# Two-layer attention with experts and feed-forward: row maxima as pairs of half-height matmuls

## The reference, cut to what matters

```python
q = (hidden_states @ Wq.T + bq).reshape(B, N, H, D).transpose(0, 2, 1, 3)
k = (encoder_hidden_states @ Wk.T + bk).reshape(B, T, H, D).transpose(0, 2, 1, 3)
...
scores = jnp.einsum('bhnd,bhtd->bhnt', q, k) * scale + attention_mask[:, None, :, :]
attn = jax.nn.softmax(scores, axis=-1)
...
attn_score = jnp.einsum('bhid,bjd->bhij', qh, k) / np.sqrt(D_HEAD)
attn_prob = jax.nn.softmax(attn_score, axis=-1)
```

## Time and profile before

| | |
|---|---|
| median of 3 runs | 789.1 us (788.37 to 789.65) |
| the profiled execution | 788.65 us, of which the span is 786.4 us |
| PE busy | 730.7 us (93%) |
| DVE busy | 645.4 us (82%) |
| ACT busy | 513.6 us (65%) |
| POOL busy | 374.3 us (48%) |
| granted TensorE clock, mean | 0.99 |
| row maxima on DVE, L342 | 256 operations, 108.6 us busy |
| row maxima on PE, L388 and mask L391 | 81.2 us and 37.7 us busy |

### The profile page before, as it was taken

The page is one execution under the profiler, slowest core; times in us unless marked ns, Lnnn a source line. Parts: engine busy times, 40 slices in busy tenths (PEclk is TensorE's granted clock), DMA queues, the critical chain, the costliest instruction groups (busy, mean ns, idle before and its releaser), DMA issues.

```text
span 786.4 us, 13553 instructions
## 1 busy us (share of the span) xinstructions
PE 730.7 (93%) x4372; PEld 548.4 (70%) x4372; DVE 645.4 (82%) x1546; ACT 513.6 (65%) x943; POOL 374.3 (48%) x323
## 2 busy tenths in 40 slices
PE   4799999999999999999998999999989999999995
PEld 3456666766558888888875555555558888888985
DVE  7658778777878878888887888998788999999995
ACT  3546556565654456555436777677778989989885
POOL 6374444334222223232214232222259999999884
PEclk9999999999999999999999999999999999999999
DMA  7975635564210000001047755755200000000001
GB/s 231 135 208 121 143 71 96 119 120 87 69 36 1 1 1 7 1 1 55 1 60 121 92 78 77 131 76 78 32 1 1 2 28 28 28 28 2 28 28 54
DMA packets 25101, 48.64 MB, mean 62 GB/s; under 512 B 3686, under 2 KB 7016, under 8 KB 24520
## 3 DMA queue, kind: packets, MB, share of 16 engines
q1 hardware_dynamic: 23366, 46.54, 30.6%
q10 hardware_dynamic: 1666, 1.24, 0.5%
HBM read 12.12 MB, written 4.19 MB: 21 GB/s over the span
## 4 chain that ended last, share of the span: by engine, by line
PE 53%; DVE 20%; issue 9%; ACT 7%; DMA 6%; POOL 4%; DVEq 0%; ACTq 0%; POOLq 0%
PE bank L141 15%; PE bank L649 7%; PE bank L413 6%; PE bank L436 6%; DMA qst<-mt 5%; PE bank L424 5%; PE bank L388 4%; DVE mx L342 4%; PE bank L416 3%; PE bank L812 3%; DVE fpart L768 3%; DVE x L617 2%; PE bank L391 2%; DVE fyl L780 2%; POOL fy L728 2%
## 5 line engine op out<-in xcount | busy, mean ns | idle before, releaser
L316 ACT ACTIVATE pt<-bank 77x512 f32<-77x512 f32 x256 | 141.0, 589 | 79.1 <-PE bank L416 59.3
L342 DVE TENSOR_REDUCE mx<-bank 128x4 f32<-128x308 f32 x256 | 108.6, 470 | 22.9 <-PE bank L391 12.3
L413 PE MATMUL bank<-qst,l_kst 128*77 128x512 f32 (+1 forms) x256 | 102.6, 416 | 16.8 <-DMA qst<-mt 10.5
L721 POOL TENSOR_TENSOR frise<-fg,fg 128x512 f32<-128x512 f32 x64 | 101.8, 1591 | 6.0 <-DVE fpart L768 0.8
L388 PE MATMUL bank<-l_kblk,qh 128*128 128x308 f32 x256 | 81.2, 339 | 7.6 <-DVE mx L342 6.4
L284 POOL TENSOR_TENSOR ol<-ot,oh 128x512 fp32r<-128x512 f32 x32 | 41.4, 1293 | 94.5 <-ACT oh L321 50.4
L103 POOL TENSOR_TENSOR rstd<-var,minus_half 128x4 f32<-128x4 f32 x32 | 34.8, 1088 | 102.5 <-DVE var L98 54.4
L617 DVE SCALAR_TENSOR_TENSOR x<-bank,eweight,x 128x256 f32<-128x256 f32 x192 | 79.5, 475 | 4.5 <-PE bank L649 4.2
L413 PEld LDWEIGHTS bank<-qst,l_kst 128*77 128x77 f32 (+1 forms) x256 | 36.5, 146 | 66.0 <-ACT pt L316 24.1
L114 ACT ACTIVATE xn<-x,shift,rstd 128x256 f32<-128x256 f32 (+1 forms) x128 | 67.0, 592 | 17.9 <-POOL shift L105 17.9
L812 PE MATMUL bank<-fw2h,fyh 128*128 128x256 f32 x256 | 73.3, 286 | 5.0 <-DVE fyl L780 4.7
(11 more groups left out here) (176 smaller groups left out, 2115.6 us busy)
## 6 DMA issues: line engine op xcount, KB each, us to landing
qst<-qh SPq DMA_DIRECT2D x64, 256.0 KB, 6.5
qst<-ql SPq DMA_DIRECT2D x32, 256.0 KB, 8.7
out<-x SPq DMA_DIRECT2D x8, 512.0 KB, 2.6
qst<-ml SPq DMA_DIRECT2D x8, 480.0 KB
x<-in_x SPq DMA_DIRECT2D x3, 1024.0 KB, 12.7
weights<-in_mlp_w SPq DMA_DIRECT2D x2, 1024.0 KB, 5.2
mraw<-in_mask SPq DMA_DIRECT2D x8, 154.0 KB
x<-in_x SPq DMA_DIRECT2D x2, 512.0 KB, 5.4
```

Of the source, the lines that this page charges most:

```text
L316: self.nc.scalar.activation(self.pt[0:T, i // 4 % 2, i % 4, :], self.bank_of(G, i)[0:T, :], ACT.Exp).then_inc(self.probs, 1)
L342: self.nc.vector.reduce_max(out, banks[u % len(banks)][:, 0:4 * T].rearrange("q (p par t) -> q p par t", p=2, par=2), AX.X).then_inc(self. ...
L413: last = self.nc.tensor.matmul(out, layer.kst[rows, layer.stack(c * HC + 2 * k + par), b * T:(b + 1) * T], self.qst[rows, self.slot(G), c ...
L721: self.nc.gpsimd.tensor_tensor(self.rise[:, k % 2, :], self.g1[:, k % self.R, :], self.g0[:, k % self.R, :], ALU.subtract).then_inc(self.r ...
```

## The change

`max_pair` replaces `max_unit`. Pair v (8 in a block) is row tile t and slab c. It makes two matmuls of 64 rows each, one on the rows 0 to 63 and one on the rows 64 to 127, each of 308 columns and 128 columns of weights, into the two banks of a double tile of PSUM. In the built program the two carry the array tile (64, 128) at row 0 and row 64; the bias row and the anchors carry (32, 128). In layer 0 two mask matmuls on all rows follow. One `reduce_max` takes both banks, 616 columns a row. There is only one double tile in the steady blocks (`X`), so pair v waits until pair v - 1 is taken; two in blocks 0 and 8. The constant `headsel` changes with the order of the heads.

The orders are new on PE, DVE and ACT. On PE in layer 0: both queries at i = 1, the weigh of the block before at i = 3 (was 1), the outputs at 11 (was 10), the third weigh at 14 (was 15), `hidden` of the experts at 12 and 15 (was 10 and 14). In layer 1: the queries of slab 0 before score 0, the weigh of the block before at i = 1, the first weigh at 6, both turns at 12. On DVE in layer 1 `fold` of slab 0 comes behind the small parts of the norm.

```diff
-        for u in units:
-            t, c, half = u // 4, u % 4 // 2, u % 2
-            dve.wait_ge(self.max_scores, 16 * G + u + 1)
...
+        for v in units:
+            t, c = divmod(v, C)
+            dve.wait_ge(self.max_scores, 8 * G + v + 1)
...
+            out = self.mx[:, t, :].rearrange("q (par c p) -> q c par p", par=2, c=C)[:, c, :, :]
+            self.nc.vector.reduce_max(out, banks[v % len(banks)][:, :, 0:4 * T].rearrange("q par (p t) -> q par p t", t=T),
                                       AX.X).then_inc(self.max_taken, 1)
...
+        if v >= len(banks):
+            pe.wait_ge(self.max_taken, 8 * G + v - len(banks) + 1)
+        pair = banks[v % len(banks)]
+        tile = slice(t * P, (t + 1) * P)
+        for par in range(2):
+            half = slice(64 * par, 64 * par + 64)
+            last = self.nc.tensor.matmul(pair[:, par, 0:4 * T], self.qh[half, c, tile],
+                                         layer.kblk[half, c % layer.kc, self.batch(G), 4 * par:4 * par + 4, :],
+                                         start=True, stop=not layer.masked)
+        if layer.masked:
+            for par in range(2):
+                last = self.nc.tensor.matmul(pair[:, par, 0:4 * T], self.mh[:, tile], self.id5[:, 0:4 * T], start=False, stop=True)
         last.then_inc(self.max_scores, 1)
...
+        self.X = (pair,)
...
+        PAIRS0 = {2: 0, 3: 1, 6: 2, 8: 4, 11: 5}
+        PAIRS1 = {1: 0, 4: 2, 6: 3, 7: 4, 10: 5, 11: 7}
+        FIRST_MAX = (double[2], double[6])
+        FIRST_MAX1 = (double[6], double[2])
...
                     if n < 2 * BLOCKS:
-                        att.take_maxima(dve, n, range(6, 10), att.X)
+                        att.take_maxima(dve, n, range(3, 4), att.X)
+                        att.rest(dve, n, 1)
+                        att.take_maxima(dve, n, range(4, 5), att.X)
...
-                    att.fold(dve, G, 0)
                     if nm <= LN_FFN:
                         for c in range(C):
                             norm.rest(dve, nm, c, att.W[c], att.xh if nm < LN_FFN else ff.xh[0], att.xl if nm < LN_FFN else ff.xl[0])
+                    att.fold(dve, G, 0)
...
-                        if i == 15:
+                        if i == 14:
                             att.weigh(pe, l0, G, 2)
-                        if i in (10, 14) and n == BLOCKS:
-                            if i == 10:
+                        if i in (12, 15) and n == BLOCKS:
+                            if i == 12:
...
+                        if i == 0 and BLOCKS < G and n < 2 * BLOCKS:
+                            att.queries(pe, l1, n, 0)
                         att.score(pe, l1, G, i)
+                        if i == 0 and G == BLOCKS:
+                            att.queries(pe, l1, n, 0)
                         if i == 1 and n < 2 * BLOCKS:
-                            for c in range(C):
-                                att.queries(pe, l1, n, c)
-                        if i == 5:
+                            att.queries(pe, l1, n, 1)
+                        if i == 6:
                             att.weigh(pe, l1, G, 0)
```

More of the change, by code:

```diff
@@ L376, in queries, with max_pair @@
         self.norm.project(self.W[c][:, :], layer.wqh, layer.wql, slice(c * P, (c + 1) * P), self.xh, self.xl).then_inc(self.q_done, 1)
-    def max_unit(self, pe, layer, G, u, banks):
-        t, c, half = u // 4, u % 4 // 2, u % 2
+    def max_pair(self, pe, layer, G, v, banks):
+        t, c = divmod(v, C)
         pe.wait_ge(self.qh_ready, C * G + c + 1)
[L381 to L388, removed]
         if layer.masked:
             pe.wait_ge(self.mask_ready, 3 * G + 1)
-            last = self.nc.tensor.matmul(bank, self.mh[:, tile], self.id5[:, 0:4 * T], start=False, stop=True)
+        if v == 0:
+            need(pe, self.mt_ready, G)
+        if v >= len(banks):
[10 more added lines that the diff above has]
+                last = self.nc.tensor.matmul(pair[:, par, 0:4 * T], self.mh[:, tile], self.id5[:, 0:4 * T], start=False, stop=True)
         last.then_inc(self.max_scores, 1)
     def turn_maxima(self, pe, G, bank):
-        pe.wait_ge(self.max_taken, 16 * (G + 1))
+        pe.wait_ge(self.max_taken, 8 * (G + 1))
         for t in range(NT):
@@ L846, in sem @@
             return stack.enter_context(nc.semaphore(n))
-        ps = [stack.enter_context(nc.psum_tensor(f"bank{i}", [P, N], F32)) for i in range(8)]
+        single = {i: stack.enter_context(nc.psum_tensor(f"bank{i}", [P, N], F32)) for i in (0, 1, 4, 5)}
+        double = {i: stack.enter_context(nc.psum_tensor(f"bank{i}{i + 1}", [P, 2, N], F32)) for i in (2, 6)}
+        ps = [single[i][:, :] if i in single else double[i - i % 2][:, i % 2, :] for i in range(8)]
         x = place.at("x", m["x"], [P, BLOCKS * NT, D], F32)
@@ L1406, in _ @@
                         att.rest(dve, n, 0)
[L1407 to L1408 removed]
+                        att.take_maxima(dve, n, range(0, 1), att.X)
                     if p >= BLOCKS:
@@ L1673, in _ @@
                         if i == 12 and n < 2 * BLOCKS:
-                            att.turn_maxima(pe, n, att.X[0])
-                        if i in (12, 13) and nm <= LN_FFN:
-                            if p >= BLOCKS:
-                                pe.wait_ge(att.added, 2 * p + i - 11)
-                            else:
-                                pe.wait_ge(att.ql_ready, C * n + i - 11)
-                            norm.turn(pe, nm, i - 12, att.W[i - 12])
+                            att.turn_maxima(pe, n, ps[2])
+                        if i == 12 and nm <= LN_FFN:
+                            for c in range(C):
+                                if p >= BLOCKS:
+                                    pe.wait_ge(att.added, 2 * p + c + 1)
+                                else:
+                                    pe.wait_ge(att.ql_ready, C * n + c + 1)
+                                norm.turn(pe, nm, c, att.W[c])
                         if i == 14:
```

149 lines of the change are left out of this document (71 added, 78 removed).

## The result

The changed kernel takes **811.6 us** (median of 4 runs, 810.12 to 813.9) against 788.89 for the kernel before (788.37 to 789.65): a ratio of 1.029, interval 1.0263 to 1.0317. The forecast said 793 and 782 to 804, so the sign is right and the loss, 22.7 us, is more than five times the 4 us forecast. The profiled execution has a span of 807.9 us against 786.4. The mean granted clock is 0.969, where it was 0.99; the prediction has no word on the clock.

What follows compares the result with a forecast made beforehand. PE was taken to bound layer 0, and PE's work plus 2.6 us of waits a block layer 1. Layer 0 at +8.8 us and layer 1 at -4.5 gave +4.3 on the 789.1 median: 793 us, range 782 to 804.

Steps and rivals of the forecast that it cites:

- For the eight pairs made ahead I take nothing: there DVE was the pace.: Stage ahead of block 0: the eight pairs made there cost no extra time, since DVE set the pace.
- I take +2: Block 0: +2 us, because no outputs lie between pairs 5, 6 and 7 and each waits for the one before.
- stays (+0.2): Block 8, first of layer 1: no outputs there either, so its length stays, at +0.2 us.
- some 1.3 us: One double tile: from a pair's start to its release by DVE, the time the next pair must wait out.
- +1.3 us in each: Layer 0, blocks 1 to 6: changes of height add 1.5 us, shorter bank waits return some 0.2; 7.8 in all.
- -0.7: Layer 1, six steady blocks: each falls from 20.52 to 19.8 us.
- the 1.5 that it was to replace: Layer 1 blocks: 1.5 us a block that PE loses at DVE's pace, waiting for its maxima, in the kernel before.
- +1.1 on paper: Layer 1 blocks: the pairs' changes of height and exposed loads add 1.1 us a block to PE's work.
- The last weigh of layer 0, -1: Last block of layer 0: the last weigh's 0.93 us idle wait for DVE's unfold goes, -1 us.
- Serial loads: Rival: the second half's weights load behind the first's, 0.11 us dearer a pair; total 802, chance 0.15.
- A height that costs nothing: Rival: changing to 64 rows is free, layer 0 about -9 us and layer 1 about -17; total 764, chance 0.05.
- layer 1 gains more: Rival: PE's waits for the double tile stay low, layer 1 gains 1.4 us a block; total about 786, chance 0.25.

Runs made afterwards that it cites:

- experiment 6: Changed kernel, each pair made ahead for block 0 issuing its two half-height matmuls twice into the same banks: 811.82 us (one run).
- experiment 8: Changed kernel, mask matmuls of block 0's pairs made ahead also at half height, part of the mask left out: 810.34 us (one run).
- experiment 9: Changed kernel, each full-height mask matmul of block 0's pairs made ahead issued twice: 816.43 us (one run).
- experiment 1: Changed kernel with both matmuls of every pair on all 128 rows; orders, double tiles and merged maxima kept: 792.4 us, ratio to before 1.0046.
- experiment 2: Changed kernel with full height only in the sixteen pairs made ahead, for blocks 0 and 8: 803.97 us, ratio 1.0188.
- experiment 3: Changed kernel with full height in the sixteen pairs made ahead and in those that blocks 0 and 8 compute: 803.67 us, ratio 1.0178.
- experiment 4: Kernel before, with only layer 1's queries of slab 0 moved ahead of score 0, ACT and DVE work matched: 783.6 us, ratio 0.9928.
- experiment 5: Kernel before, with the queries of slab 0 ahead of score 0 in both layers: 781.2 us, ratio 0.9896.
- experiment 7: Kernel before, with the 16 units of block 8 sharing one bank instead of two, all at full height: 799.88 us, ratio 1.0142.

## Why the prediction was wrong

**The sentence that failed first: "For the eight pairs made ahead I take nothing: there DVE was the pace."** It is +5.4 us. At full clock the sentence held, by a hair: a pair takes PE 0.82 us and DVE about 0.8, and in the changed kernel PE still waits 0.41 us for DVE ahead of the third pair (23.31). At half clock PE became the pace and the values behind it lasted nearly twice as long. All four kernels with half-height matmuls in this stage (the changed one, experiments 6, 8 and 9) spent 17 to 30 us at half clock before block 0's first score, and all that have full height there (before, experiments 1 to 5 and 7) at most 4.5. That the height of the pairs decides how long the clock stays down is shown by experiment 2, which alters nothing else there. That the clock falls at all isn't the height's alone: in this stage it fell in all four runs with half height (21.0 to 24.1), and also in experiment 1, one of seven with full height, where it was down for 3.4 us. What it is about the half height that counts is open: not the changes of height alone (experiment 8), not how long the halves run or how much full-height work lies between (6 and 9), each seen in one run. Nor is it settled why, in the runs with half height, the clock stays low through the values, which have none of it; in experiments 1 to 3 the same matmuls run at full clock.

**Block 0, "I take +2": +4.4.** With all at full height 1.4 remain (experiments 1 and 3). They go with the waits for the one double tile: PE waits for DVE's maxima for 2.5 us in this block in the changed kernel and in experiments 1 to 3, for 0.3 before. The other 3.0 go with the height: 1.45 as in a steady block by experiment 1, and about 1.5, the remainder, for more time at half clock: 8.6 us of the block (65.1 to 71.9, and the end of the first stretch) against 3.3 in experiment 1.

**Block 8, "stays (+0.2)": +5.1.** PE's timeline of the changed kernel, four of its eight pairs:

```profile
441.56 0.41 PE L393 MATMUL bank<-l_kblk,qh 64*128 64x308 f32 x2
442.95 0.41 PE L393 MATMUL bank<-l_kblk,qh 64*128 64x308 f32 x2 [0.99 <-DVE mx L343]
...
449.09 0.41 PE L393 MATMUL bank<-l_kblk,qh 64*128 64x308 f32 x2
450.48 0.41 PE L393 MATMUL bank<-l_kblk,qh 64*128 64x308 f32 x2 [0.98 <-DVE mx L343]
```

And DVE's between them:

```profile
442.01 0.80 DVE L343 TENSOR_REDUCE mx<-bank 128x8 f32<-128x616 f32 x1 [0.66 <-PE bank L393]
443.40 0.80 DVE L343 TENSOR_REDUCE mx<-bank 128x8 f32<-128x616 f32 x1 [0.59 <-PE bank L393]
```

A pair starts, DVE begins 0.45 us later, works 0.80, and PE starts the next 0.14 after that: 1.39 us, with PE and DVE idle in turn. The working had this chain ("some 1.3 us") and used it for layer 1's steady blocks and block 0, where other work lies between pairs; in block 8 there are no outputs to put there, and the text dropped it. PE's waits for DVE in this block rose from 0.9 to 2.9 us, and 6.8 us of it ran at half clock (450.8 to 457.6), which costs up to 3.4. Full height for its own pairs doesn't help (23.4 and 22.1 in experiments 1 and 3), and one bank in the kernel before brings such a fall of the clock too (experiment 7). So one buffer is shown to be enough to bring such a loss; that it is the whole cause here isn't shown, since a second double tile in the changed kernel's block 8 was not tried.

**Layer 0's steady blocks, "+1.3 us in each": +1.56.** The price of the height, 1.5, is right to 0.05 (1.45). The 0.2 of short waits was not given back: at full height the new order and the merged maxima still make the block 0.1 longer than before (24.43 against 24.32).

**Layer 1's steady blocks, -0.7: -0.46 in most, -0.41 on the mean** (one of the six got longer, 20.9 after 20.7). Here two terms were off, in opposite directions. PE's waits in blocks 9 to 14, first of the changed kernel:

```profile
PE bank L393 <- DVE mx L343: 6.0, 13, 0.6
PE bank L141 <- DVE xl L136: 0.6, 1, 0.6
```

then of experiment 1, at full height:

```profile
PE bank L393 <- DVE mx L343: 8.6, 18, 0.8
```

The wait for `qst<-mt` is gone as foreseen (5.5 us in the earlier trace rows), and 6.0 in six blocks is the 1.0 a block that was forecast. But the 1.5 that it was to replace is 3.9 / 6 = 0.65 by the earlier trace rows and 0.65 again in experiment 4. I had measured the two in different ways: the 1.5 from distances of starts (0.86 lost in a stretch whose row shows 0.36 us of idle time), the 1.0 as idle time alone. Counted alike, one double tile adds waits (0.65 to 1.4 at full height) instead of saving 0.5. On the other side the changes of height, +1.1 on paper, cost 0.20 (20.07 against 19.87 in experiment 1), since PE spends most of that time where it would wait anyway. The account of a block: 20.53, less 1.05 for the border (experiment 4), plus 0.39 for one double tile with the merged maxima and what else differs in the order (experiment 1 against 4, not told apart), plus 0.20 for the height: 20.07.

**DVE.** All maxima of the changed kernel, by lines:

```profile
L343 DVE TENSOR_REDUCE mx<-bank 128x8 f32<-128x616 f32 x128 | 101.5, 796 | 52.4 <-PE bank L398 35.3 <-PE bank L393 14.4
```

101.5 us instead of 108.6, 7 of the 8 us foreseen, and no time of the kernel is seen to come from it: DVE was idle for 52.4 us ahead of them, nearly all of it for PE (22.9 us before).

**The last weigh of layer 0, -1.** PE's timeline of the changed kernel, the third and the last weigh:

```profile
245.44 1.07 PE L431 MATMUL bank<-pt,l_vall 128*32 128x512 f32 x8 [0.80 <-DVE ut L348]
...
248.44 1.06 PE L431 MATMUL bank<-pt,l_vall 128*32 128x512 f32 x8
```

The last one no longer waits, as foreseen. But the third, now one score earlier, waits 0.80 us for DVE, where it waited for nothing before (227.73 there): the wait only moved. The part from block 7 on is 0.2 us shorter in all.

**The rivals.** Serial loads (802, the first in the list, which the text above it calls the second) came nearest in time, but its mechanism isn't there: the halves load at once. "A height that costs nothing" is dead by the rows of the isolated pair, and "layer 1 gains more" by its -0.46; that rival's 786 also counts seven blocks, though only six have the border that it gains from. None named the clock. Of 17.2 us missed, 5.4 lie in the start, 4.9 in block 8, 2.4 in block 0, and the steady blocks of the two layers hold 1.5 and 1.8; the rest, 1.2, is the last weigh and the 0.5 promised for the pairs made ahead for layer 1.

## What to carry to other kernels

Two matmuls of half height side by side save the time of one, and pay for the change and then an exposed load, each way (here twice 0.09 and twice 0.10 us, against 0.14 saved). An estimate from these: at full clock they would pay from three pairs in a row between full ones, 0.42 against 0.38. No run here has such a row, and in this kernel half height in one stage also went with a clock at half. Merging two buffers into one larger one halves DVE's instructions and also the buffers in flight; look at the blocks with the least other work between the uses (here 0 and 8), and price what it does to TensorE's clock as well as the wait. When a change bundles several edits, try the smallest alone: the border order by itself was worth 0.7% in one layer and 1.0% in both, and the bundle hid it under a loss of 2.9%.

## What the hardware showed that I had not expected

- A granted clock of 0.50 for 24 us on end (24.1 to 48.0) with PE busy for 23.1 of them, in and behind half-height matmuls (experiment 9: 34.1 us, busy for 33.2). With PE busy for only 4.55 of 6.00 us at full height the clock was 1.00; with the same 4.55 at half height, 0.50. PE's busy share alone doesn't tell the clock.
- In experiment 7 the clock fell to half for 13.7 us in the middle of 13 waits for one buffer at full height, none over 0.7 us and 6.6 us in all.
- Two half-height weight loads of 128 columns last 0.19 us together, as one full one does; two full ones last 0.30.
- In layer 1 a pair's changes of height, 0.2 us and more on PE's own account, came to 0.20 for a whole block of eight pairs; PE's waits for DVE there are 6.0 us in six blocks with half height and 8.6 without.
